# A gated attention and LoRA block on one core: the transposes of the middle tiles move from TensorE to transposing DMAs

## The reference

```python
def fake_quant(x, scale, zp):              # s = 8/255, z = 128
    q = clip(round(x / s + z), 0, 255)
    return (q - z) * s
...
x = x + tanh(g_xattn) * matmul(fake_quant(layernorm(x)), fake_quant(ctx))   # x (2,1024,2048), ctx (2,2048,2048)
h = layernorm(x)                           # rows again normalised
logits = h @ Wr.T                          # 4 experts
gates = softmax over the two largest logits
mid = einsum('tf,erf->ter', h, A)          # rank 16
x = x + tanh(g_ffn) * sum_e gates * (mid @ B) * 4
```

## Time and profile before

| | us |
|---|---|
| median of 3 runs (lowest, highest) | 429.81 (429.75, 431.95) |
| the profiled execution: its time, its span | 432.26, 430.5 |
| TensorE busy, share of the span | 360.3, 84% |
| VectorE | 334.7, 78% |
| ScalarE | 257.6, 60% |
| GpSimd | 85.5, 20% |
| mean granted TensorE clock | 0.949 of 2.4 GHz |

### The profile page before, as it was taken

The page is one execution under the profiler, slowest core; times in us unless marked ns, Lnnn a source line. Parts: engine busy times, 40 slices in busy tenths (PEclk is TensorE's granted clock), DMA queues, the critical chain, the costliest instruction groups (busy, mean ns, idle before and its releaser), DMA issues. The chain is left out here.

```text
span 430.5 us, 7428 instructions
## 1 busy us (share of the span) xinstructions
PE 360.3 (84%) x2480; PEld 213.2 (50%) x2480; DVE 334.7 (78%) x764; ACT 257.6 (60%) x240; POOL 85.5 (20%) x74
## 2 busy tenths in 40 slices
PE   0063549679989998989899999999999999999954
PEld 0031224265555555555556464756565656565642
DVE  2549994897897979797979787879787878687584
ACT  1655698377859587776767455556464655555140
POOL 1000000130404030222222222222222222224020
PEclk9996779868999999999999999999999999999995
DMA  4999980246755645556472222222222222312022
GB/s 142 344 402 428 424 311 4 97 142 246 251 162 180 190 159 202 185 189 201 150 240 99 99 99 98 99 98 97 97 97 97 97 97 97 99 50 97 2 97 99
DMA packets 22241, 68.52 MB, mean 159 GB/s; under 512 B 3204, under 2 KB 3716, under 8 KB 20100
## 3 DMA queue, kind: packets, MB, share of 16 engines
q1 hardware_dynamic: 22216, 68.20, 44.4%
HBM read 51.42 MB, written 16.78 MB: 158 GB/s over the span
## 5 line engine op out<-in xcount | busy, mean ns | idle before, releaser
L539 PE MATMUL ps_main<-q,q1T 128*128 128x512 f16 x928 | 213.3, 381 | 0.0
L539 PEld LDWEIGHTS ps_main<-q,q1T 128*128 128x128 f16 x928 | 88.1, 99 | 101.9 <-issue 8.5
L404 ACT ACTIVATE h_hi<-x,small_tile 128x1024 f16<-128x1024 f32 x32 | 39.4, 1234 | 65.5 <-DVE small_tile L830 65.5
L349 POOL TENSOR_TENSOR h_lo<-work,h_hi 128x1024 f16<-128x1024 f32 x31 | 66.6, 2148 | 43.7 <-ACT work L409 41.9
L814 DVE SCALAR_TENSOR_TENSOR x<-ps_main,small_tile,xt 128x512 f32<-128x512 f32 x60 | 44.8, 747 | 23.8 <-DMA out_x<-x 14.5
L788 DVE BATCH_NORM_STATS2 small_tile<-xt 128x6 f32<-128x512 f32 x64 | 40.8, 683 | 16.8 <-DMA xt<-in_x 16.7
L343 POOL TENSOR_TENSOR small_tile<-small_tile 128x1 f32<-128x1 f32 x16 | 8.8, 549 | 210.3 <-DVE small_tile L826 210.3
L392 ACT ACTIVATE work<-xt,small_tile 128x1024 uint8<-128x1024 f32 x32 | 38.1, 1234 | 16.0 <-DVE small_tile L804 16.0
L819 DVE BATCH_NORM_STATS2 small_tile<-x 128x6 f32<-128x512 f32 x64 | 44.3, 692 | 1.7
L888 DVE TENSOR_TENSOR x<-ps_delta,x 128x512 f32<-128x512 f32 x64 | 42.3, 683 | 2.7 <-PE ps_delta L605 2.7
L382 ACT ACTIVATE ctx_stage<-ctx_stage,small_tile 128x1024 uint8<-128x1024 f32 x32 | 38.7, 1236 | 5.0 <-DMA ctx_stage<-in_ctx 5.0
(11 more groups left out here) (98 smaller groups left out, 401.9 us busy)
## 6 DMA issues: line engine op xcount, KB each, us to landing
xt<-in_x SPq DMA_DIRECT2D x32, 512.0 KB, 3.7
q<-in_ctx SPq DMA_DIRECT2D x16, 1024.0 KB, 17.8
ctx_stage<-in_ctx SPq DMA_DIRECT2D x32, 512.0 KB, 5.0
out_x<-x SPq DMA_DIRECT2D x64, 256.0 KB, 2.2
x<-in_L_ffn_A SPq DMA_DIRECT2D x1, 512.0 KB
x<-in_L_ffn_B SPq DMA_DIRECT2D x1, 512.0 KB, 15.9
small_tile<-in_L_xattn_x_scale SPq DMA_DIRECT2D x2, 0.5 KB, 4.2
small_tile<-in_L_xattn_x_zp SPq DMA_DIRECT2D x2, 0.5 KB, 4.7
```

Of the source, the lines that this page charges most:

```text
L349: nc.gpsimd.tensor_tensor(h_lo[:, h, :], work[:, h, :], h_hi[:, h, :], ALU.subtract).then_inc(h_lo_ready, 1)
L404: nc.scalar.activation(h_hi[:, h, :], x1[:, b % 2, half(h)], ACT.Identity, bias=h_bias[:, :], scale=h_rstd[:, :]).then_inc(h_hi_ready, 1)
L539: mm = pe.matmul(acc[:, :], q1T[:, b % 2, k, :], q2[:, batch(b), k, cols(n)], start=(k == 0), stop=(k == KT - 1))
```

## The change

From slot 1 to slot 15 the transposes of TensorE into PSUM and the copies out of PSUM are gone: h_hi, h_lo (tiles 0 to 14) and the codes of x (tiles 2 to 15) are each transposed by two DMAs of 128 x 1024 float16 (256 KB) from SBUF straight into hT or q1T. SyncE issues them, on the queue of all other DMAs, six in a slot. Only tiles 0 and 1 (codes) and the last tile (h) still go through TensorE. In TensorE's list mid_hi moves ahead of product 2, where turn_hi stood, and mid_lo stands alone between products 2 and 3.

```diff
+            def turn_q1(b, i, h):
+
+                wait(sp, x_rounded, b, i, 2, h + 1)
...
+                wait(sp, main_done, b, i, NB, -NB)
...
+                sp.dma_start_transpose(q1T[:, b % 2, h * HK:(h + 1) * HK, :], q1_code[:, h, :]).then_inc(q1T_loaded[h], 16)
+
+            def turn_hi(b, i, h):
+
+                wait(sp, h_hi_ready, b, i, 2, h + 1)
...
+                wait(sp, lo_used, b, i, 2, h - 1)
...
+                sp.dma_start_transpose(hT[:, h, :, :], h_hi[:, h, :]).then_inc(hiT_loaded[h], 16)
+
+            def turn_lo(b, i, h):
+
+                wait(sp, h_lo_ready, b, i, 2, h + 1)
...
+                wait(sp, hi_used, b, i, 2, h + 1)
...
+                sp.dma_start_transpose(hT[:, h, :, :], h_lo[:, h, :]).then_inc(loT_loaded[h], 16)
...
                 if 3 <= b < TILES - 1:
                     load_x(b + 1, i, 1)
-                if b >= 2:
-                    store_out(b - 2, i, (2, 3))
+                turn_hi(b - 1, i, 0)
+                ctx_half(0)
+                turn_hi(b - 1, i, 1)
+                store_out(b - 2, i, (2, 3))
                 if b < TILES - 2:
                     load_x(b + 2, i, 0)
...
+                turn_lo(b - 1, i, 0)
+                turn_lo(b - 1, i, 1)
+                if b < TILES - 1:
+                    turn_q1(b + 1, i, 0)
+                    turn_q1(b + 1, i, 1)
                 ctx_half(1)
                 ctx_half(2)
                 ctx_half(3)
...
-                wait(pool, lo_turned, b, i, 2, h - 1)
+                wait(pool, loT_loaded[h], b, i, 16, 0)
...
             def high_part(b, i, h):
                 wait(act, h_bias_ready, b, i, 1, 1)
-                wait(act, hi_turned, b, i, 2, h - 1)
+                wait(act, hiT_loaded[h], b, i, 16, 0)
+                wait(act, h_lo_ready, b, i, 2, h - 1)
...
             def normal_half(b, i, h):
-                wait(act, q1_turned, b, i, 2, h + 3)
+                if b == 0:
+                    act.wait_ge(q1_turned, h + 3)
+                else:
+                    wait(act, q1T_loaded[h], b, i, 16, 0)
...
-                copy_hiT(b - 1, i, 0)
-                copy_hiT(b - 1, i, 1)
                 if ahead:
                     scale_x(b + 1, i, 0)
                     scale_x(b + 1, i, 1)
-                copy_loT(b - 1, i)
                 scale(3)
                 gate_exp(b - 1, i)
-                if ahead:
-                    copy_q1T(b + 1, i, 0)
-                    copy_q1T(b + 1, i, 1)
...
                         main(b, i, 1, general)
-                        turn_hi(b - 1, i, 0)
-                        turn_hi(b - 1, i, 1)
+                        mid_hi(b - 1, i, 0)
+                        mid_hi(b - 1, i, 1)
                     main(b, i, 2, general)
...
-                    for h in range(2):
-                        mid_hi(b - 1, i, h)
-                        turn_lo(b - 1, i, h)
-                    for h in range(2):
-                        mid_lo(b - 1, i, h)
-                        if b < TILES - 1:
-                            turn_q1(b + 1, i, h)
+                    mid_lo(b - 1, i, 0)
+                    mid_lo(b - 1, i, 1)
                     main(b, i, 3, general)
...
                 if ahead:
                     round_x(b + 1, i, 1)
-                copy_loT(b - 1, i)
                 stats_h(b, i, 2)
```

More of the change, by code:

```diff
@@ L543, in main, with turn_last @@
                 mm.then_inc(main_done, 1)
[L545 to L548 removed]
+            def turn_last(h, src, turned):
                 for k in range(HK):
@@ L580, in mid_lo @@
             def mid_lo(b, i, h):
-                wait(pe, loT_ready[h], b, i, 1, 1)
+                if b == TILES - 1:
+                    pe.wait_ge(loT_ready[h], 1)
+                else:
+                    wait(pe, loT_loaded[h], b, i, 16, 16)
                 for k in range(HK):
```

122 lines of the change are left out of this document (68 added, 54 removed).

## The result

| | us |
|---|---|
| changed kernel, median of 4 runs (lowest, highest) | 500.45 (499.31, 501.26) |
| kernel before, 4 runs on the same chip | 430.88 (429.75, 432.57) |
| ratio, 95% interval | 1.161 (1.157 to 1.165) |
| the profiled execution: its span; before | 498.7; 430.5 |
| mean granted TensorE clock; before | 0.870; 0.949 |

What follows compares the result with a forecast made beforehand. TensorE was taken as the bound, with a hardly slower chain through VectorE, the x load and h_lo. Slots 3 to 8 (+6.9), 9 to 13 (+2.95) and the end slots gave 7.75, say +8, on 429.81: 438 us, range 420 to 480.

Steps and rivals of the forecast that it cites:

- TensorE is the bound, 2.70 us a tile to win: Second-half tile: TensorE busy all 21.06 us; dropping six half transposes at 0.45 us would leave it 18.36.
- X = 1.0: Time in us for which one 256 KB transposing DMA keeps the queue, estimated from half a 512 KB x load's transfer.
- the forecast's own slope of 23 us: Change of the total time for each us of a transpose's queue time, from 2 x 11 slots and a little.
- The load of x keeps the queue until it lands: On SyncE's shared queue, h_lo's transposes wait behind the x load, which lands 3.1 us after issue.
- not held: Rival: transposes are not held behind the load of x, engines work on both; 420 us, chance 0.18.
- 12.30 us from addition to load: Second-half cycle term: from product 3's addition on VectorE to SyncE's issue of the half 0 x load, 302.75 to 315.05.
- 3.77 us from product 3 to its addition: Second-half cycle's last term: from product 3's start on TensorE to its addition on VectorE.
- the clock falls: Rival: idle time before mid_lo drops TensorE to 1.2 GHz, doubling product 3; 44 us more, 482 us, chance 0.08.
- First half, 23.95 us: Predicted first-half cycle between additions of product 3, through the x load and h_lo; 1.15 us over 22.80.
- The other waits have cover: Waits besides h_lo's cost nothing; h_hi half 1, about 2 us later behind a ctx load, only moves idle time from mid_lo.
- Slot 1, +0.5: Slot 1 as a latency chain, each transpose and copy replaced by a DMA's: win 1 or lose 3, taken as +0.5 us.
- The codes have over 4 us of slack: Transposed codes are needed only at the next product 0, over 4 us after mid_lo, and land in time.

Runs made afterwards that it cites:

- all moves: Changed kernel with transposing DMAs one slot later, h_lo before the x load, first ctx load behind both, half 1 of x before stores from slot 7: 443.56 us.
- h_lo alone: Kernel before with only h_lo by transposing DMA, here with the matmuls on h_hi moved ahead of product 2: 492.52 us, ratio 1.144.
- Filling the idle time: Changed kernel with 512-column matmuls, results unused, added where TensorE stands idle before the matmuls on h_hi and h_lo: 485.41 us, ratio 1.123.
- h_hi alone: Kernel before with only h_hi (tiles 0 to 14) by transposing DMA, its matmuls staying behind product 2: 455.48 us, ratio 1.058.
- h_lo before x: Changed kernel with the two transposes of h_lo issued before the load of half 0 of x: 477.79 us, ratio 1.105.

## Why the prediction was wrong, point by point

The sum beside the two profiled spans; a period runs from reduce to reduce, is named by the slot in which it ends, and goes into the row of the forecast's slots:

| | forecast | measured |
|---|---|---|
| slot 1 | +0.5 | +17.6, of which 15.5 after the first h_hi |
| slot 2 | +0.3 | +3.5 |
| slots 3 to 8 | +6.9 | +25.3 |
| slots 9 to 13 | +2.95 | +20.6 |
| slot 14 | -1.1 | +1.55 |
| slot 15 and the tail | -1.8 | -0.3 |

The direction of the whole was right; the size failed in every row, and for several reasons.

**TensorE is the bound, 2.70 us a tile to win.** Right as a ceiling. With all moves the second half reaches 18.91 us of TensorE busy in a period of 19.79; the prediction had 18.36 for TensorE alone.

**X = 1.0.** Mis-sized: 1.37 alone, (5.97 - 3.1) / 2 = 1.43 in the kernel with h_lo alone, 1.66 by the queue's share in the changed kernel. By the forecast's own slope of 23 us this is 9 to 15 us. The x load's 2 us of transfer were about right; halving them with the bytes was the error: a transpose costs the engines what a load of twice its bytes costs. The 261 GB/s of the Trainium skill ("DMA: Bandwidth & Descriptors", "Latency and other measured facts") gave the same 1.0 and isn't borne out: 256 KB in 1.37 us is 191 GB/s. A smaller slip is the 14 us of loads and stores in a period of the first half: by the earlier trace rows they are 0.55 x 22.80 = 12.5; it moved neither the sum nor a chance.

**The load of x keeps the queue until it lands.** Right enough in effect: a transpose 0.37 us behind a load lands 4.5 us after the load's issue, 3.1 + 1.37 by the forecast's rule, and half 1 of h_lo comes after 5.97 us in the kernel with h_lo alone, 5.84 by the rule. As a mechanism it is not strict: the two slow each other, the transpose by 1.1 us and the load by 0.45. The rival "not held" is refuted: the move of h_lo ahead of the load gave 18 to 24 us.

**12.30 us from addition to load.** This step failed. It was taken over from the trace of before, as if a transpose issued behind the other load of x left that load alone. The load took 5.4 us, VectorE waited 3.30 and the term became 14.23. The kernel that issues this load earlier took the periods of the second half from 25.3 to 23.6.

**3.77 us from product 3 to its addition.** This step failed too, by the rival that had 0.08, "the clock falls". After 3.53 us of idle time, eight matmuls and 0.34 us more the clock stood at 0.52 and the term became 5.45. The argument against it, that product 2 runs right before, did not hold. Filling the idle time gave 11 to 16 us; what the clock costs besides can't be read from that, since the fill also takes time. It adds to a cycle that is already closed by DMAs: each wait that grows makes the next matmuls slower, so the terms aren't independent, as the sum had them.

**First half, 23.95 us.** Measured 26.0 to 27.4, and by another path than the forecast's. Its cycle closed through the load of x and h_lo; the kernel's closed through h_hi, for which TensorE waited 4.57 us in the tile shown against 0.29 for h_lo. The step that failed is "The other waits have cover": the prediction gave half 1 of h_hi "about 2 us more" for the transfer of the ctx load ahead of it and took them as idle time moved from mid_lo. It didn't count that load's wait for codes of ctx, which held SyncE, nor product 2 behind the idle time at the lower clock. The ctx load moved away by itself gave 7 us.

**Slot 1, +0.5.** The largest miss in one slot: 15.5 us, and 3.5 in the period behind it. The prediction compared latencies of single steps there and didn't list what stands ahead of the first transpose in SyncE's list, ctx loads that wait for VectorE.

**The codes have over 4 us of slack.** Right: alone they cost nothing, and without slot 1's loss they gain.

**What would show it.** Four of the signs spoke: mid_hi was the main wait (58.8 us against 29.4; the prediction took that for X over 2, but X was under 1.7 and SyncE's list was the reason), the clock stood at 0.5 in tiles, TensorE's busy time fell by only 8.8 us (its matmuls ran longer at the lower clock), and periods were 25 and 27. The range's top, 480, was 20 us short. That the sign came out was not mere luck: h_lo behind the load of x does cost time, as its move showed. But most of the 70 us came from steps that the forecast had at nothing or nearly so.

What stays open: how much of the timed differences is start-up; how the 24.4 us periods of the first half, with all moves, divide between full DMA engines and the waits of SyncE, why the period after slot 1 stays at 28.97 there, and where half of the loss with h_hi alone comes from.

## What to carry to other kernels

When a DMA joins an in-order queue, list what stands ahead of its first issue and between its halves, with what each of those waits for, and price what it does to the transfer just ahead of it (in slot 1 the wait ahead was 10.5 us, a transpose's own share of the engines 1.37). Replace on-chip work by DMAs where the result is needed late, and put those that are needed soon ahead of loads that aren't. Where a change leaves TensorE a new idle stretch (here 3 us in a tile), work out the time with the matmuls behind it at 1.2 GHz as well.

## What the runs showed of the hardware

- A transposing DMA of 128x1024 float16 makes 1056 packets, lands in 3.0 us alone, takes 1.37 us of the 16 engines (a plain copy of the same bytes 0.70) and holds its issuer 1.24 us; in slot 1 of the changed kernel, with the queue loaded, two issues held SyncE 7.67 us. In a series of four, landing included, a transpose took 1.8 us, a plain copy 1.1.
- A load was slowed by the DMA issued right behind it, from 3.0 to 3.4 or 3.6 us, by a transpose and a plain copy alike.
- Start-up, up to the first h_hi, differed by up to 8.6 us between profiled executions of programs that do the same work until then; that is more than most single gains here.
- A second queue for loads did not speed them where the engines were busiest: in the first half they landed in 7.0 us beside transposes and ctx loads, 4.6 on one queue.
- In the changed kernel TensorE was at 1.2 GHz for most of 4 us after waits of 3.5 and 0.3 us with eight matmuls between them. With h_lo before x it was at full clock after two waits of 0.8 to 0.9 us in slot 10, and yet fell to 0.50 (432 to 434 us) behind two waits of 0.86 and 0.97 us in slot 14. So these runs give no safe length for a wait.
